# Order of the value-stage matmuls and the planner's time grid in a transformer layer with head-wise attention

## What is computed

```python
q = x @ Wq + bq                                  # 16 heads of 64
kv = (x @ Wdown + bdown) @ Wup + bup             # latent of 256, then k and v of 16 heads
q, k = apply_rope(q), apply_rope(k)              # B,T,H,D -> same rotation for q and k of a token
att = softmax(einsum('bthd,btgd->bthg', q, k) / 8)
out = einsum('bthg,btgd->bthd', att, v) @ Wout + bout
x = layernorm(x + out)
h = silu(x @ wg.T / 127) * (x @ wu.T / 127)      # hidden size 3072
y = layernorm(x + (h @ wd.T / 127))
```

## Time and profile before

| | us |
|---|---|
| median of 2 runs | 3694.19 |
| lowest and highest run | 3666.02, 3722.36 |
| the profiled execution, slowest core | 3664.43 |
| its span, first to last instruction (core 3) | 3662.6 |
| spans of the 8 cores | 3617.5 to 3662.6 |
| mean granted TensorE clock of the cores | 0.897 to 0.911 |
| PE busy (modelled) | 2735.6 |
| DVE busy | 1665.5 |
| ACT busy | 786.9 |

### The profile page before, as it was taken

How to read it: one execution, slowest core, us unless ns; L and a number is a source line. 1 busy time by engine, 2 the same in 40 slices (tenths; PEclk the granted TensorE clock), 3 DMA queues, 4 the chain that set the end, 5 groups by cost and what they waited for, 6 DMA issues and landing times.

```text
span 3662.6 us, 41194 instructions; the slowest of 8 cores (3617.5 to 3662.6 us)
## 1 busy us (share of the span) xinstructions
PE 2735.6 (75%) x12416; PEld 1087.8 (30%) x12416; DVE 1665.5 (45%) x2454; ACT 786.9 (21%) x1349; POOL 292.1 (8%) x540
## 2 busy tenths in 40 slices
PE   0001686779887989698978987798879887989566
PEld 0000222223332333233333333333323332333222
DVE  1221445355445544554546454555455436544312
ACT  0000310133123221413041303231232114130201
POOL 0112000001100110011000100011001100110010
PEclk9999856689998999989988999899989988999788
DMA  6887100202322223213231224123312322132222
GB/s 186 240 242 201 29 1 23 58 18 65 98 76 65 64 90 85 71 52 90 67 98 38 78 81 105 34 64 98 81 61 65 92 67 70 56 89 73 91 75 84
DMA packets 108701, 303.92 MB, mean 83 GB/s; under 512 B 16192, under 2 KB 24768, under 8 KB 108496
## 3 DMA queue, kind: packets, MB, share of 16 engines
q1 hardware_dynamic: 61520, 169.14, 15.8%
q0 software_dynamic: 46976, 132.15, 12.5%
HBM read 269.77 MB, written 39.85 MB: 85 GB/s over the span
## 4 chain that ended last, share of the span: by engine, by line
PE 58%; DVE 11%; DMA 9%; issue 7%; ACT 4%; DVEq 0%; ACTq 0%; POOLq 0%; POOL 0%; SPq 0%
PE P L448 10%; PE P L763 9%; PE P L405 8%; PE P L395 8%; PE P L779 8%; PE P L671 6%; DVE p_sb L730 4%; DMA wgb<-wg_s 3%; DMA wub<-wu_s 3%; PE P L344 2%; DVE esum L702 2%; PE P L817 2%; DMA wqb<-wq_s 2%; DVE hadb L646 1%; PE P L613 1%
## 5 line engine op out<-in xcount | busy, mean ns | idle before, releaser
L730 DVE TENSOR_TENSOR p_sb<-P,vdup_all 128x512 bf16<-128x512 f32 x1024 | 689.9, 689 | 601.0 <-PE P L779 465.5
L395 PE MATMUL P<-x_bf,wgb 128*128 128x512 bf16 x1536 | 511.0, 405 | 112.1 <-DMA wub<-wu_s 91.1
L763 PE MATMUL P<-e_sb,selz_sb 16*128 16x512 bf16 x1024 | 438.5, 435 | 165.5 <-DVE p_sb L730 91.8
L405 PE MATMUL P<-x_bf,wub 128*128 128x512 bf16 x1536 | 515.6, 402 | 18.5 <-DVE h_sb L421 18.5
L779 PE MATMUL P<-p_sb,id_sb 128*128 128x256 bf16 x2048 | 495.1, 306 | 27.6 <-DVE p_sb L730 21.4
L448 PE MATMUL P<-h_sb,wdb 128*128 128x512 bf16 x1536 | 489.1, 390 | 12.5 <-DVE r_bf L457 12.5
L646 DVE TENSOR_TENSOR hadb<-q_sb,krep 128x2048 bf16<-128x2048 bf16 x256 | 309.3, 1224 | 385.0 <-PE P L671 296.1
L671 PE MATMUL P<-hadb,selred_sb 128*16 128x256 bf16 x2048 | 318.0, 274 | 45.4 <-DVE hadb L646 20.2
L311 PE MATMUL P<-x_bf,wd_sb 128*128 128x512 bf16 x128 | 37.2, 443 | 356.2 <-DMA x_bf<-xt 356.0
L735 ACT ACTIVATE avn<-P 128x256 bf16<-128x256 f32 x128 | 49.1, 383 | 1053.1 <-PE P L779 1044.8
L414 ACT ACTIVATE s_sil<-P 128x512 bf16<-128x512 f32 x192 | 114.5, 596 | 720.9 <-PE P L395 720.3
(11 more groups left out here) (69 smaller groups left out, 1913.4 us busy)
## 6 DMA issues: line engine op xcount, KB each, us to landing
wdb<-wdn_s SPq DMA_DIRECT2D x64, 768.0 KB, 4.5
wgb<-wg_s POOLq DMA_DIRECT2D x192, 256.0 KB, 3.0
wub<-wu_s POOLq DMA_DIRECT2D x192, 256.0 KB, 3.0
wob<-wout_s SPq DMA_DIRECT2D x128, 256.0 KB, 3.0
wqb<-wq_s SPq DMA_DIRECT2D x64, 256.0 KB, 3.0
yt<-x2b SPq DMA_DIRECT2D x64, 256.0 KB, 2.0
stg<-wg SPq DMA_DIRECT2D x24, 512.0 KB, 5.0
stg<-wu SPq DMA_DIRECT2D x24, 512.0 KB, 5.2
```

The source lines that it names most:

```text
L395: e.matmul(o, l, r, start=st, stop=sp)),
L405: e.matmul(o, l, r, start=st, stop=sp)),
L730: add('V', (lambda e, o=o, a=a, b=b: e.tensor_mul(o, a, b)), waits=w, inc=s_v, d=640)
L763: e.matmul(o, l, r, start=True, stop=True)),
```

## The change

Two edits. In `plan_av` the hand-written order of the 24 matmuls of one J is replaced by a regular one, and the position formulas that other instructions' waits use follow it. The order before is b0 b1 b2 g0 g1 b3 g2 g3 **b4 b5 g4 g5 g6 g7 b6 b7 g8** to g15. The order after is b0 b1 b2 g0 g1 b3 g2 g3 **b4 g4 g5 b5 g6 g7 b6 g8 g9 b7 g10 g11** g12 to g15. Nothing is added or removed: the same 24 matmuls, 8 TT and one evacuation with the same waits. In the planner the grid of `es` goes from 800 ns to 400 ns, for all engines and both chains.

```diff
-                AVSCHED = ([('b', 0), ('b', 1), ('b', 2), ('g', 0), ('g', 1),
-                            ('b', 3), ('g', 2), ('g', 3), ('b', 4), ('b', 5),
-                            ('g', 4), ('g', 5), ('g', 6), ('g', 7),
-                            ('b', 6), ('b', 7)] +
-                           [('g', g) for g in range(8, NH)])
-                pos_b, pos_g = {}, {}
-                for k2, (kind2, idx2_) in enumerate(AVSCHED, 1):
-                    (pos_b if kind2 == 'b' else pos_g)[idx2_] = k2
-                pe_bcast = lambda J, gp: pe0 + J * 24 + pos_b[gp]
-                pe_gsum = lambda J, g: pe0 + J * 24 + pos_g[g]
+                pe_bcast = lambda J, gp: pe0 + J * 24 + (gp + 1 if gp < 3 else 3 * (gp - 1))
+
+                def pe_gsum(J, g):
+                    m = g // 2
+                    return pe0 + J * 24 + (3 * m + 4 + (g % 2) if g < 12 else 21 + (g - 12))
...
                 for J in range(XC):
+                    sched = [('b', 0), ('b', 1), ('b', 2), ('g', 0), ('g', 1)]
+                    for gp in range(3, 8):
+                        sched += [('b', gp), ('g', 2 * (gp - 2)), ('g', 2 * (gp - 2) + 1)]
+                    sched += [('g', 12), ('g', 13), ('g', 14), ('g', 15)]
                     first = True
-                    for kind, idx2 in AVSCHED:
+                    for kind, idx2 in sched:
...
-                key = (round(es / 800.0), -CP[id(nd)], es)
+                key = (round(es / 400.0), -CP[id(nd)], es)
```

## The result

| | before | after |
|---|---|---|
| median us (runs) | 3669.4 (8) | 3504.7 (9) |
| profiled execution: span of the slowest core | 3662.6 | 3494.0 |
| mean granted clock of the cores | 0.897 to 0.911 | 0.933 to 0.940 |

The ratio is 0.956, 95% interval 0.954 to 0.957: 4.4% faster, some 165 us.

What follows compares the result with a forecast made beforehand. It took PE-DVE waits to bound the first tile and a nearly full PE the values of tiles 1 to 7. Terms summed to -123 us from 3664.4, giving 3541; with 20 added for the median, 3560, range 3480 to 3715.

Steps and rivals of the forecast that it cites:

- scores 0 with the sums: Tiles 1 to 7: feed-forward matmuls moved into these two stretches cost +32 us in scores 0, +14 in the sums.
- First tile, -17: Values of the first tile: shorter DVE waits gain 1.0 to 1.1 us for each of 16 J, -17 us.
- F leave the values: Tiles 1 to 7: 40 feed-forward matmuls (F) leave the values, 32 to the sums, 8 to scores 0; -60 us.
- Sums stretch, +2 a tile: Sums before values 0, tiles 1 to 7: h products in DVE's queue delay the scaling and b0, +14 us.
- Shorter waits, -94: Values of tiles 1 to 7: two of three PE-DVE trips a J lie under other matmuls, 13.4 us a tile.
- Switches, +22: Values of tiles 1 to 7: one more run of b a J, 0.2 us each, +22 us; bounds 0 and 45.
- Clock, -20: Values 0 of tiles 1 to 7: F in the sums shrink the low-clock part, -20 us; bounds 0 and -90.
- Grid, 0: The planner's 400 ns grid: priced at nothing, between -45 us at best and +45 at worst.
- no gain beyond the first tile's: Rival, chance 0.27: PE's in-order queue meets the next wait at once and the sums stretch stays empty; 3669 us.
- DVE's queue gets the wait: Rival, chance 0.15: h products in scores 0 and the sums hold up DVE's queue, delaying values 0; 3770 us.
- The clock comes up too: Rival, chance 0.08: first tile's values and all of values 0 run at full clock; 3433 us, worst switch term 3480.

Runs made afterwards that it cites:

- wide b: The kernel after, with b given a 128-row operand (rows 16 to 127 zero): 3332.2 us, ratio 0.907 of the kernel before.
- before_wide_both: The kernel before (old order, old grid), with b and r both given 128x128 stationary operands: 3450.1 us, ratio 0.939.
- wide_both: The kernel after, with b and r both given 128x128 stationary operands: 3282.0 us, ratio 0.892 of the kernel before.
- new_cp_up: The kernel after, each TT counting 141 ns more in the planner's longest path, so F return to the values: 3588.4 us, ratio 0.979.
- fill_first_j: The kernel before, with sixteen idle matmuls in the first J of values 0 in tiles 1 to 7: ratio 1.002.
- wide_both_cpup70: wide_both, each TT counting 70 ns more in the planner's longest path, so F go back into the values: ratio 0.898.

## Why the prediction was right, and where its terms were off

The direction, the mechanism and the range held; 3504.7 us is 55 below the forecast of 3560, in the lower part of 3480 to 3715. The sum stood at 3541 for the profiled execution, and the profiled execution after took 3495.9, so the gain was larger than the terms: 169 us for 123. Adding 20 us for the median was wrong too; with eight runs the median before is 3669, next to the profiled execution. The terms were further off than the total: three of them (the waits, the clock, and scores 0 with the sums) missed by some 25 to 40 us, and not all to the same side, so that the total came this near is in part luck.

- **First tile, -17.** 83.3 and 83.1 us to 75.0 in both halves, -16.4. A J of 9.50 us against 9.4 to 9.5 expected.
- **F leave the values.** The count from the planner's costs, 136 a half, was met: 133 and 135. Where they went was not: of 46 F that left both stretches on the mean, about 15 went into the sums stretch (9 to 24), not 32, and 16 into scores 0 (5 to 21), not 8; the rest went to the k and v stretch and beside the output projection. Scores 0 got 3.9 us longer (4.6 expected for it).
- **Sums stretch, +2 a tile.** Wrong sign: 12.9 to 10.7. With scores 0 it makes +1.8 us a tile, 12 us in all, where I had +46 for the two. The stretch begins at the end of the last r, and as scores 0 are longer, DVE does part of the sums during them (24 DVE instructions of the stretch in the earlier trace rows, 19 after).
- **Shorter waits, -94.** Right cause, too large. By the table of work and rest the order alone, on one grid, takes 3.3 and 4.2 us from the two stretches with F as before, and 5.1 and 3.9 with F moved. That is 7.5 to 9 us a tile in place of 13.4, some -53 to -63. I had no term for the other side: F that leave uncover waits, +1.1 to 1.4 us in values 1.
- **Switches, +22.** Within its bounds. In PE's queue the runs of b rise from 862 to 942; 48 of these 80 are in tiles 1 to 7, 10 us at 0.2 each.
- **Clock, -20.** Mis-sized by more than half. The first two J of values 0 went from 25.6 to 18.8 us, 7 us a tile, but that holds a part of the shorter waits. Between kernels of the same order and grid the rest of values 0 falls by 6.4 and 8.5 us, -45 to -60 in all. I had its cause half right: the filled sums stretch matters, and so does a filled first J, which the earlier start of F also brings.
- **Grid, 0.** A gain of 15 to 27 us.

Of the rivals, "no gain beyond the first tile's" fell on the wait term and on the clock. "DVE's queue gets the wait" did happen in one sense: waits of h products for PE rose from 172.0 us to these, in the waits of the kernel after,

```profile
DVE h_sb L421 <- PE P L405: 287.3, 91, 12.8
```

but the sums stretch got shorter, and from the first r of scores 0 to the start of values 0 it is only 1.8 us longer than before (36.4 for 34.7 us on the mean of tiles 1 to 6). "The clock comes up too" came true in values 0 and not in the first tile, which stayed at 0.50; it took a wide b to lift that. The 3480 us given for this case with the switch term at its worst adds that term of 45 us to a sum that already held 22 of it; it should read 3456.

The rule on tiling modes in the Trainium skill (TensorEngine Tiling (Array Packing), Key Properties), that a change of mode drains TensorE, agrees with the 0.1 us a side that the rows show; that these 0.1 us are a drain, no run shows. Removing the changes of shape, with the clock that this brought, gave more than the whole change under study. The drain of about 1380 ns that the skill adds to a table load (ScalarE: Activation LUTs, What ACT_TABLE_LOAD costs) is not there in the trace of the kernel before. ACT in its scores 1 of tile 3:

```profile
1660.09 1.28 ACT L414 ACT_TABLE_LOAD   x1
1661.38 0.60 ACT L414 ACTIVATE s_sil<-P 128x512 bf16<-128x512 f32 x1
1661.99 1.28 ACT L658 ACT_TABLE_LOAD   x1
1663.29 0.46 ACT L658 ACTIVATE e_sb<-P,cvec_sb 16x256 bf16<-16x256 f32 x1
```

From the start of one load to the Exp behind the next are 3.20 us, and the two loads and the Silu make 3.16 of them. So a load costs 1.28 us here, and the 10 to 19 us more that the prediction worked out from the page's rule don't arise.

## What to carry to other kernels

In a queue that runs in order, put an instruction that waits on the newest result behind the ones that only need the one before it, and give a round trip between engines one whole step of other work to hide under. When a planner mixes two chains by longest path, a shorter path in one moves the other chain's work to other stages, so count what lands where, and look for stretches that run empty and drag the clock down after them. And before ordering small matmuls cleverly, look at whether padding them with zeros to their neighbours' shape removes the cost that the order was managing.

## What the hardware did that I had not expected

- A matmul with 16 rows beside ones with 128 costs 0.1 us on each side, and the same matmul padded with zero rows costs nothing extra (0.21 to 0.22 between starts).
- The granted clock in a stretch of b and g alone is 0.50 with 16-row b, and 0.96 with 128-row b of which 112 rows are zeros, in the new order; in the old order it is 0.50 and 0.64. Number and columns of the matmuls are the same. It isn't the faster pace that lifts it: the kernel after runs a J in 9.50 us at 0.50 and stays there, while before_wide_both runs its first J slower, in 10.1 us at 0.50, and its second at 0.84:

```profile
450.00:460.00 10.00, 7.60 (x24) 2.88 (x24) 5.18 (x9) 0.36 (x1) 0.00 (x0) 0.50 0.01 2
460.00:468.60 8.60, 5.62 (x25) 2.41 (x24) 5.25 (x8) 0.15 (x2) 0.00 (x0) 0.84 0.00 1
```

Whether it is the rows or the missing changes of shape, no run tells apart.
- wide_both shows a third level. On one die of its profiled execution (cores 4 to 7) the clock is 0.81 for 250 to 300 us, and these cores end 24 us later than the other die's. The same level stands in the traces of new_cp_up (59 to 137 us on one die), of fill_first_j (8 to 14 us on one die) and of wide_both_cpup70 (273 us and more on every core). Core 6, a stretch of 100 us:

```profile
2900.00:3000.00 100.00, 94.59 (x433) 45.25 (x441) 53.36 (x83) 9.25 (x18) 1.82 (x4) 0.81 0.23 73
```

That PE is 95% busy there is what it has in common with other stretches that ran at 1.00, so what sets this level is open. The Trainium skill (TensorE: Matmul & The Clock Gate, Seeing it yourself) has it as a peak-current limit of 13/16 for dies on which three cores or more run dense matmuls; the level agrees, but most of this run's dense stretches, and all in the traces of the kernels before and after, ran without it.
